# Scores of four pairs of heads in one burst of TensorE, and a new order of steps

## Chip, cores and metric

One core of one Trainium2 chip runs the whole program. The metric is the device time of one execution in microseconds (us).

## What is computed

Four layers in a row over x of shape (8, 1024, 256), fp32, each with a residual and a plain layer norm in front:

```python
x = x + attention_block(layernorm(x))   # 16 heads of 16, window of 128; inside: layer norm, qkv, attention, w_o, then an MLP with gelu
x = x + rwkv_ffn(layernorm(x))          # sigmoid(xr Wr) * (relu(xk Wk)^2 Wv)
x = x + mamba(layernorm(x))             # in_proj, causal conv of 4 taps, silu, selective scan over 16 states of 512 channels, gate, out_proj
x = x + top1_moe(layernorm(x))          # one of 8 experts for each of the 8 sequences, 256 -> 1024 -> 256
```

The change touches the sliding-window attention. With chunks of 128 rows, queries of a chunk see the keys of the chunk before and of their own:

```python
scores = jnp.einsum('bhcqd,bhckd->bhcqk', qc, kcat) * scale   # 128 x 256 for each head and chunk
scores = jnp.where(valid, scores, -inf)                       # band mask
attn = softmax(scores); out = einsum('bhcqk,bhckd->bhcqd', attn, vcat)
```

## The kernel before

The 8 sequences are cut in two groups of 512 tokens, so 16 groups `i` pass through the stages head, attention, mlp, rwkv, middle (what stands ahead of the scan), scan, back (out_proj and norm), route, fetch (weights of the expert from HBM) and expert. Groups overlap: while group i is in attention, i-1 is in mlp, rwkv and middle, i-2 in scan, i-3 in back and i-4 in expert.

Every engine has a generator for each stage, cut in steps by `yield`. `run` goes through one list, `order`, and lets each engine do its part of each step. So the order of work is the same on all five instruction queues, and only semaphores hold an engine back. The list comes from `schedule` (line 114): `COSTS` gives each step a length, `THREADS` places chains of stages in a time counted in slots (one group a slot), with `lag`, begin and end; all steps are sorted by that time. `SCAN_PERIOD` is the number of scan steps in a slot: the scan has `SCAN_STEPS` = 145 of them, one tile every two steps, so scans of neighbouring groups overlap a little.

`banks_of` (line 142) then goes through the order and gives each use of a PSUM bank (`uses_of`: name, first and last step) the bank that has been idle longest. There are 8 banks. PE waits for a bank with `free(use)`, readers wait with `full(use)`, and `gone(use)` says that it was read.

Attention has 72 beats from step `ATT0` = 14. A group has 4 chunks of 8 pairs of heads, 32 pairs n. Pair p of a chunk has its queries and keys in rows 32*(p%4) to 32*(p%4)+31 of `q_own` and `kT`, so a score matmul has 32 rows of contraction; `q_own` holds each pair twice, with the other head's rows zero (`par` 0 and 1). Before, `scores_of(v)` (line 487) makes pairs 2v and 2v+1 at beat 4v, in two banks: four matmuls, par 0 of both and then par 1 of both (line 499). On VectorE `masked(n)` (line 1065, the instruction stands at line 1074) adds the band, writes `prob` and the row's maximum and gives the bank back; at beats 4v+1 and 4v+2. ScalarE's `exponentials` (line 791) follow, then PE turns the probabilities (`turn`, line 511), ScalarE copies them (line 783), PE makes the values (line 527), and GpSimd's `divide` (line 1420). `prob` has a ring of 3 slots: `masked(n)` waits until `turn(n - 3)` is done.

The scan: SP loads a tile of u (line 1620, ring of 12 slots) and of delta (line 1607, ring of 5), each 256 KB, at step 2k + 10 + `LOAD_AT`; POOL multiplies by B (line 1499, `INPUT_AT`), ACT makes the decay in a bank (line 962, `DECAY_AT`), DVE scans (line 1287), POOL multiplies by C (line 1506, `OUT_AT`), and PE sums four tiles at once (line 670) at `SUM_AT`. `load_u(k)` waits until the sums of tile k - 12 are done, `load_delta(k)` until the decay of tile k - 5 is. u and delta come from the middle stage by way of DRAM: SP stores them (`store_delta`, lines 1577 and 1579) in middle's steps 22, 24, 26 and 28, in the same queue as the loads; each store waits for DVE's product (line 1255) and ACT's copy (line 937). At the start of mlp, PE transposes normed rows (`zb`, line 460), ACT copies them (`nb`, line 749) and PE makes the hidden rows (line 466).

## Time and profile before

| | |
|---|---|
| runs (us) | 3621.44, 3627.49, 10848.22; median 3627.49 |
| profiled execution (us) | 3620.18 |
| its span from first to last instruction (us) | 3618.1 |
| mean granted clock of TensorE | 0.910 of full speed |
| instructions | 58031 |
| DMA | 736.59 MB, mean 204 GB/s |

A row of a group of instructions names line, engine, operation, tiles written and read, shapes and count; then busy time in us (overlapping instructions counted once), mean length of one in ns, and the engine's idle time just before them with what ended most of it. PE is TensorE's matmul side, PEld its weight loads, DVE is VectorE, ACT ScalarE, POOL GpSimd, SP SyncE, which issues all DMAs of this kernel. An fp32 matmul stands in the trace as two MATMUL instructions. The chain of work that ended last is followed back from the last instruction, at each step to what released it.

### The profile page before, as it was taken

Reading aid. Unit: us, or ns where it says so; the run is one execution under the profiler, and the core shown is the slowest. Engines: PE = TensorE matmul, PEld = TensorE weight load, DVE = VectorE, ACT = ScalarE, POOL = GpSimd, SP = SyncE. Lnnn points to the kernel's source line nnn. Section 1 sums busy time; section 2 is a strip of 40 time slices with the busy share of each in tenths; the row PEclk is TensorE's granted clock in tenths of the full one; section 3 lists DMA queues with packets and bytes.
Section 4 is the critical chain, followed back from the end, with each engine's and each line's share of the span. In section 5 each row is a group of like instructions: output and inputs, shape, how many; then the busy total and the mean of one; then the engine's idle time right before and its main releaser. Section 6 shows DMA issues by size and latency. Waiting matters only on the chain.

```text
span 3618.1 us, 58031 instructions
## 1 busy us (share of the span) xinstructions
PE 3042.8 (84%) x17392; PEld 1885.8 (52%) x17392; DVE 2583.2 (71%) x5920; ACT 2415.5 (67%) x5331; POOL 2786.8 (77%) x2583
## 2 busy tenths in 40 slices
PE   5888888897988979899898989889898998987557
PEld 3555454464655646465464646556464654644236
DVE  3356878687787868778686876878687776878870
ACT  4577767676776857677685767768576776855431
POOL 1117989898887979888897988889798888977880
PEclk9998898899999989999898989989898998988678
DMA  2017877877777877877777887778878778789981
GB/s 73 7 42 192 214 208 193 225 215 238 207 204 222 217 229 216 241 209 204 223 218 228 220 237 210 207 222 226 230 215 234 210 204 231 213 248 256 284 235 37
DMA packets 423337, 736.59 MB, mean 204 GB/s; under 512 B 53427, under 2 KB 100147, under 8 KB 423027
## 3 DMA queue, kind: packets, MB, share of 16 engines
q1 hardware_dynamic: 423026, 732.89, 72.3%
q8 instruction: 142, 2.33, 0.3%
q14 instruction: 169, 1.38, 0.1%
HBM read 648.84 MB, written 83.89 MB: 203 GB/s over the span
## 4 chain that ended last, share of the span: by engine, by line
PE 60%; ACT 9%; POOL 9%; DVE 9%; issue 6%; DMA 5%; SPq 2%; ACTq 0%; DVEq 0%; POOLq 0%
PE bank L466 16%; PE bank L474 9%; PE bank L589 6%; PE bank L499 6%; PE bank L736 5%; PE bank L722 5%; PE bank L511 5%; POOL u_rows L1506 4%; PE bank L670 4%; DMA u_rows<-u_dram 3%; PE bank L527 3%; POOL u_rows L1499 3%; DVE u_rows L1287 3%; ACT prob L791 2%; DMA d_rows<-delta_dram 1%
## 5 line engine op out<-in xcount | busy, mean ns | idle before, releaser
L1506 POOL TENSOR_TENSOR u_rows<-u_rows,c_rows 128x512 f32<-128x512 f32 x1024 | 1304.8, 1277 | 169.3 <-DVE state L1292 116.4
L1499 POOL TENSOR_TENSOR u_rows<-u_rows,b_rows 128x512 f32<-128x512 f32 x960 | 1225.8, 1278 | 71.8 <-DMA u_rows<-u_dram 70.8
L962 ACT ACTIVATE bank<-d_rows,a_rep 128x512 f32<-128x512 f32 x1024 | 697.7, 688 | 296.5 <-DMA d_rows<-delta_dram 150.6
L1287 DVE TENSOR_TENSOR_SCAN u_rows<-bank,state,u_rows 128x512 f32<-128x512 f32 x512 | 644.0, 1271 | 83.3 <-ACT bank L962 78.9
L1287 DVE TENSOR_TENSOR_SCAN u_rows<-bank,u_rows 128x512 f32<-128x512 f32 x512 | 622.8, 1216 | 85.0 <-ACT bank L962 81.2
L791 ACT ACTIVATE prob<-prob,neg_max 128x256 f32<-128x256 f32 x1024 | 509.9, 505 | 42.9 <-DVE neg_max L1074 42.7
L670 PE MATMUL bank<-u_rows,sum_n 128*32 128x512 f32 x2048 | 309.1, 679 | 237.9 <-POOL u_rows L1506 235.0
L1074 DVE CUSTOM_DVE_ANT_0 prob<-bank,band 128x256 f32<-128x256 f32 x896 | 337.6, 416 | 178.0 <-PE bank L499 159.8
L511 PE MATMUL bank<-ident,prob 128*128 128x128 f32 x2048 | 330.3, 290 | 89.0 <-ACT prob L791 70.8
L511 PEld LDWEIGHTS bank<-ident,prob 128*128 128x128 f32 x2048 | 247.0, 148 | 230.8 <-issue 185.1
L499 PE MATMUL bank<-kT,q_own 32*128 32x256 f32 x2048 | 299.9, 412 | 47.4 <-DVE neg_max L1074 25.1
L466 PE MATMUL bank<-nb,w 128*128 128x512 f32 x512 | 271.1, 663 | 63.9 <-ACT nb L749 63.9
L499 PEld LDWEIGHTS bank<-kT,q_own 32*128 32x128 f32 x2048 | 181.9, 190 | 186.4 <-issue 135.7
L722 PE MATMUL bank<-y4T,w 128*128 128x256 f32 x1024 | 256.8, 398 | 10.7 <-DMA e_b<-in_b 9.6
L783 ACT ACTIVATE nT<-bank 128x512 f32<-128x512 f32 x256 | 151.2, 591 | 166.6 <-PE bank L527 128.3
L466 PE MATMUL bank<-nb,w_in 128*128 128x512 f32 x512 | 246.4, 609 | 15.0 <-DVE u_rows L1287 6.2
L736 PE MATMUL bank<-w,eT 128*128 128x256 f32 x1024 | 236.3, 384 | 6.3 <-ACT eT L1024 6.2
L722 PEld LDWEIGHTS bank<-y4T,w 128*128 128x128 f32 x1024 | 195.7, 200 | 67.1 <-issue 19.9
L589 PE MATMUL bank<-w,region_b 128*128 128x256 f32 x1024 | 230.4, 381 | 0.0
L670 PEld LDWEIGHTS bank<-u_rows,sum_n 128*32 128x32 f32 x2048 | 42.6, 113 | 352.8 <-POOL u_rows L1506 267.3
L736 PEld LDWEIGHTS bank<-w,eT 128*128 128x128 f32 x1024 | 191.3, 190 | 62.0 <-issue 33.7
L466 PEld LDWEIGHTS bank<-nb,w 128*128 128x128 f32 x512 | 103.3, 212 | 203.3 <-issue 134.6
(167 smaller groups left out, 5276.4 us busy)
## 6 DMA issues: line engine op xcount, KB each, us to landing
u_rows<-u_dram SPq DMA_DIRECT2D x1024, 256.0 KB, 5.4
d_rows<-delta_dram SPq DMA_DIRECT2D x1024, 256.0 KB, 5.1
w<-in_W SPq DMA_DIRECT2D x28, 1024.0 KB, 7.2
zs_dram<-region_b SPq DMA_DIRECT2D x64, 256.0 KB, 2.8
xc_dram<-region_b SPq DMA_DIRECT2D x64, 256.0 KB, 2.5
u_dram<-region_b SPq DMA_DIRECT2D x64, 256.0 KB, 3.4
delta_dram<-region_b SPq DMA_DIRECT2D x64, 256.0 KB, 3.1
yg<-xc_dram SPq DMA_DIRECT2D x64, 256.0 KB, 4.9
```

The lines of the kernel that those rows point to most:

```text
L466: ins = e.matmul(banks[use.bank][0:rows, :], lhsT(n), rhs(n), start=(n == 0), stop=(n == parts - 1))
L499: ins = e.matmul(banks[at.bank][:, 256 * par:256 * par + 256], q_own[rows, k, par, c * P:(c + 1) * P], kT[rows, k, c * P:(c + 2) * P], sta ...
L511: ins = e.transpose(banks[at.bank][:, (2 * par + half) * P:(2 * par + half + 1) * P], prob[:, n % PROBS, par, half * P:(half + 1) * P], id ...
L589: ins = e.matmul(banks[at.bank][:, 0:D], hT[:, k, t * P:(t + 1) * P], w_2[:, k, :], start=(k == 0), stop=(k == KF - 1))
L670: ins = e.matmul(banks[at.bank][32 * q:32 * q + 32, :], sum_n[:, r, :], rows_of(i, 4 * b + q), start=(r == 0), stop=(r == 3), skip_group_c ...
L722: ins = e.matmul(banks[at.bank][:, m % 2 * 256:m % 2 * 256 + 256], w_1[:, n, m * P:(m + 1) * P], y4T[:, n, t0:t0 + 256], start=(n == 0), s ...
L736: ins = e.matmul(out, eT[:, k, j * P:(j + 1) * P], w_2[:, k, :], start=(k == 0), stop=(k == KM - 1))
L791: ins = e.activation(tile, tile, ACT.Exp, scale=-1.0, bias=neg_max[:, c % 2, h:h + 1], accum_out=den[:, c % 2, h:h + 1])
L962: e.activation(banks[at.bank][:, :], delta_of(i, k), ACT.Exp, scale=a_rep[:, j:j + 1]).then_inc(filled[at.bank], 1)
L1287: e.tensor_tensor_scan(rows, banks[at.bank][:, :], rows, state[:, k:k + 1] if i % 2 else 0.0, ALU.mult, ALU.add).then_inc(drained[at.bank], 1)
L1499: e.tensor_tensor(rows, rows, b_rows[:, :], ALU.mult).then_inc(bx_ready.sem, 1)
L1506: e.tensor_tensor(rows, rows, c_rows[:, :], ALU.mult).then_inc(hc_ready.sem, 1)
```

## The change

`scores_of(u)` now makes four pairs 4u to 4u+3 at beat 8u, in four row groups and four banks: eight matmuls, par 0 of the four and then par 1. The masks of the four stand at beats 1, 2, 3 and 6 behind it (`MASK_AT`). `schedule` and `banks_of` become one function: at each turn it takes the earliest step whose banks are idle and whose chain's forerunners are through, so a step that needs more banks than are idle is put behind others. The costs of steps, the places of the chains and three numbers of the scan (`SCAN_PERIOD`, `LOAD_AT`, `SUM_AT`) are new. Instructions, sizes and buffers are otherwise the same.

```diff
--- before.py
+++ after.py
@@ -37,36 +37,37 @@
 
 
 ATT0, PROBS, TURNED, QUAD = 14, 3, 4, 4
+MASK_AT = (1, 2, 3, 6)
 AFTER = ATT0 + 72
 
 
 TILES = 64
-SCAN0, LOAD_AT, INPUT_AT, DECAY_AT, KEEP_AT, OUT_AT, SUM_AT, GATE_AT = 10, -9, -4, -2, 1, 3, 6, 8
+SCAN0, LOAD_AT, INPUT_AT, DECAY_AT, KEEP_AT, OUT_AT, SUM_AT, GATE_AT = 10, -10, -4, -2, 1, 3, 7, 8
 GATE_LOAD_AT = 14
 SCAN_STEPS = SCAN0 + 2 * (TILES - 1) + GATE_AT + 1
 
-SCAN_PERIOD = 133
+SCAN_PERIOD = 136
 COSTS = {
     "head": [2] * 6,
-    "attention": [1.5] * 2 + [0.8] * (ATT0 - 2) + [1] * (AFTER - ATT0) + [1.5] + [2] * 4,
-    "mlp": [1.5] * 2 + [1] * 16 + [4] + [1] * 8 + [2.5] * 3,
+    "attention": [1.5] * 2 + [0.8] * (ATT0 - 2) + [1] * (AFTER - ATT0) + [1.5] + [1.57] * 4,
+    "mlp": [1.5] * 2 + [1] * 8 + [1.31] * 8 + [4] + [0.92] * 8 + [1.75] * 3,
     "rwkv": [1.5] * 5 + [1] * 11 + [1.5] + [2.5] * 3,
     "middle": [1.5] * 2 + [1] * 27,
     "scan": [1] * SCAN_STEPS,
-    "back": [1.5, 1, 1, 1, 1, 1.5, 1.5, 1.5, 1, 1],
+    "back": [2.5] + [1] * 4 + [1.5] * 3 + [1] * 2,
     "route": [1] * 3,
     "fetch": [1],
-    "expert": [1] * 25,
+    "expert": [1] * 12 + [1.06] * 13,
 }
 
 
 THREADS = (
     (("head", "attention"), 0, 0.0, 1.0),
     (("mlp", "rwkv", "middle"), 1, 0.0, 1.0),
-    (("scan",), 2, 0.05, 0.05 + SCAN_STEPS / SCAN_PERIOD),
-    (("back",), 3, 0.16, 0.35),
-    (("route",), 3, 0.36, 0.39),
-    (("fetch",), 4, 0.39, 0.40),
+    (("scan",), 2, 0.034, 0.034 + SCAN_STEPS / SCAN_PERIOD),
+    (("back",), 3, 0.173, 0.368),
+    (("route",), 3, 0.378, 0.408),
+    (("fetch",), 4, 0.408, 0.418),
     (("expert",), 4, 0.44, 0.97),
 )
 
@@ -84,7 +85,7 @@
         for n in range(32):
             v, odd = divmod(n, 2)
             at = ATT0 + 4 * v
-            out += [(f"s{n}", at, at + 1 + odd), (f"p{n}", at + 5 + odd, at + 6 + 2 * odd)]
+            out += [(f"s{n}", ATT0 + 8 * (n // 4), ATT0 + 8 * (n // 4) + MASK_AT[n % 4]), (f"p{n}", at + 5 + odd, at + 6 + 2 * odd)]
             if n % 4 == 0:
                 out.append((f"a{n // 4}", ATT0 + 2 * n + 13, ATT0 + 2 * n + 14))
         return out + [("o0", AFTER, AFTER + 1), ("o1", AFTER, AFTER + 1)]
@@ -111,35 +112,32 @@
     return []
 
 
+class Use:
+
+
+
+    def __init__(self, bank, n, f):
+        self.bank, self.n, self.f = bank, n, f
+
+
 def schedule(batches):
 
-    at = []
+
+
+    chains = {}
     for thread, (stages, lag, begin, end) in enumerate(THREADS):
         total = sum(sum(COSTS[stage]) for stage in stages)
         for i in range(2 * batches):
-            spent = 0.0
+            chain, spent = [], 0.0
             for stage in stages:
-                if stage == "route":
-                    if i % 2 == 0:
-                        continue
-                    which = i // 2
-                else:
-                    which = i
+                if stage == "route" and i % 2 == 0:
+                    continue
+                which = i // 2 if stage == "route" else i
                 for step, cost in enumerate(COSTS[stage]):
-                    at.append((i + lag + begin + (end - begin) * spent / total, thread, stage, which, step))
+                    chain.append((i + lag + begin + (end - begin) * spent / total, thread, stage, which, step))
                     spent += cost
-    return [(stage, which, step) for _, _, stage, which, step in sorted(at, key=lambda s: s[:2])]
-
-
-class Use:
-
-
-
-    def __init__(self, bank, n, f):
-        self.bank, self.n, self.f = bank, n, f
-
-
-def banks_of(order, batches):
+            if chain:
+                chains[thread, i] = chain
 
     begins, ends = {}, {}
     for stage in COSTS:
@@ -147,17 +145,37 @@
             for name, first, last in uses_of(stage, shared):
                 begins.setdefault((stage, shared, first), []).append(name)
                 ends.setdefault((stage, shared, last), []).append(name)
-    idle, counted, signalled, uses = list(range(8)), [0] * 8, [0] * 8, {}
-    for stage, i, step in order:
-        shared = stage == "scan" and shared_inputs(i, batches)
-        for name in begins.get((stage, shared, step), ()):
+
+    def earlier(thread, i):
+
+        out = [] if THREADS[thread][0] == ("scan",) else [(thread, i - 1)]
+        if thread:
+            out.append((thread - 1, i | 1 if THREADS[thread][0] == ("fetch",) else i))
+        return out
+
+    order, uses = [], {}
+    idle, counted, signalled = list(range(8)), [0] * 8, [0] * 8
+    while chains:
+        for key, chain in sorted(chains.items(), key=lambda c: c[1][0][:2]):
+            _, _, stage, i, step = chain[0]
+            shared = stage == "scan" and shared_inputs(i, batches)
+            names = begins.get((stage, shared, step), ())
+            if len(names) <= len(idle) and not any(c in chains for c in earlier(*key)):
+                break
+        else:
+            raise AssertionError("no bank is idle")
+        order.append((stage, i, step))
+        for name in names:
             bank = idle.pop(0)
             uses[stage, i, name] = Use(bank, counted[bank], signalled[bank])
             counted[bank] += 1
             signalled[bank] += not (stage == "scan" and name[0] == "y")
         for name in ends.get((stage, shared, step), ()):
             idle.append(uses[stage, i, name].bank)
-    return uses
+        del chain[0]
+        if not chain:
+            del chains[key]
+    return order, uses
 
 
 def build_block_stack(nc, d):
@@ -184,8 +202,7 @@
     EL = P // NS
     assert WINDOW == P and SEQ % G == 0 and HD == 16 and GROUPS == 2 and ED // EL == TILES and KE * 16 == TILES
 
-    order = schedule(BATCH)
-    uses = banks_of(order, BATCH)
+    order, uses = schedule(BATCH)
 
     with ExitStack() as ctx:
         def sb(name, shape, dt=F32):
@@ -484,15 +501,15 @@
             def use(name):
                 return uses["attention", i, name]
 
-            def scores_of(v):
-
-                if v == 0:
+            def scores_of(u):
+
+                if u == 0:
                     for name in ("q0", "q1", "k0", "k1"):
                         e.wait_ge(*gone(use(name)))
-                for n in (2 * v, 2 * v + 1):
+                for n in range(4 * u, 4 * u + 4):
                     e.wait_ge(*free(use(f"s{n}")))
                 for par in range(2):
-                    for n in (2 * v, 2 * v + 1):
+                    for n in range(4 * u, 4 * u + 4):
                         c, p = divmod(n, PAIRS)
                         k, q = divmod(p, 4)
                         at, rows = use(f"s{n}"), slice(32 * q, 32 * q + 32)
@@ -548,8 +565,8 @@
                 yield
                 yield
             for beat in range(AFTER - ATT0):
-                if beat % 4 == 0 and beat < 64:
-                    scores_of(beat // 4)
+                if beat % 8 == 0 and beat < 64:
+                    scores_of(beat // 8)
                 v, at = divmod(beat - 5, 4)
                 if at < 2 and 0 <= v < 16:
                     turn(2 * v + at)
@@ -1105,9 +1122,9 @@
                 if n == 0:
                     yield
             for beat in range(AFTER - ATT0):
-                v, at = divmod(beat, 4)
-                if at in (1, 2) and v < 16:
-                    masked(2 * v + at - 1)
+                u, at = divmod(beat, 8)
+                if at in MASK_AT and u < 8:
+                    masked(4 * u + MASK_AT.index(at))
                 if beat % 8 == 2 and beat >= 10 and beat < 72:
                     reciprocals((beat - 10) // 8)
                 yield
```

## Rows read from the trace of the kernel before

**Rows 1.** The page: span, and busy time (share of it) and instructions of each engine

```profile
span 3618.1 us, 58031 instructions
...
PE 3042.8 (84%) x17392; PEld 1885.8 (52%) x17392; DVE 2583.2 (71%) x5920; ACT 2415.5 (67%) x5331; POOL 2786.8 (77%) x2583
```

**Rows 2.** Busy time by stretch (us), two whole periods

```profile
core 0: us, PE busy (x) PEld busy (x) DVE busy (x) ACT busy (x) POOL busy (x), PEclk, DMA share, GB/s
1773.00:1985.00 212.00, 186.74 (x1086) 116.61 (x1085) 159.11 (x339) 150.22 (x333) 178.94 (x167) 0.93 0.76 219
1985.00:2196.00 211.00, 188.02 (x1095) 117.04 (x1095) 158.11 (x391) 150.21 (x333) 178.32 (x163) 0.93 0.80 221
```

**Rows 3.** Busy time by stretch, one period: while scores are made, and the rest

```profile
1139.00:1253.00 114.00, 105.71 (x743) 73.17 (x744) 94.83 (x270) 86.22 (x228) 101.19 (x95) 0.96 0.81 217
1253.00:1351.00 98.00, 78.44 (x345) 42.29 (x345) 63.22 (x121) 63.86 (x106) 76.26 (x68) 0.90 0.73 221
```

**Rows 4.** Chain that ended last, by line: stretch 1139 to 1253, then the whole span

```profile
by line: PE bank L499 12.4%; PE bank L589 12.3%; PE bank L722 11.2%; PE bank L511 10.3%; PE bank L466 9.5%; PE bank L527 6.9%; PE bank L736 6.5%; PE bank L474 6.4%; PE bank L670 6.1%; issue 4.5%; ACT prob L791 2.3%; ACT region_b L879 2.0%; 
...
by line: PE bank L466 15.6%; PE bank L474 9.1%; issue 6.3%; PE bank L589 6.2%; PE bank L499 5.5%; PE bank L736 5.2%; PE bank L722 4.9%; PE bank L511 4.5%; POOL u_rows L1506 4.1%; PE bank L670 3.8%; DMA u_rows<-u_dram 3.3%; PE bank L527 3.3%
```

**Rows 5.** Timeline of PE (start us, us, what): one score step, whole and by starts

```profile
1194.14 1.13 PE L499 MATMUL bank<-kT,q_own 32*128 32x256 f32 x8
...
1194.46 0.38 PE L499 MATMUL bank<-kT,q_own 32*128 32x256 f32 x2
...
1194.68 0.38 PE L499 MATMUL bank<-kT,q_own 32*128 32x256 f32 x2
...
1194.89 0.38 PE L499 MATMUL bank<-kT,q_own 32*128 32x256 f32 x2
...
1195.20 0.33 PE L511 MATMUL bank<-ident,prob 128*128 128x128 f32 x1
```

**Rows 6.** Groups of instructions by form: score matmuls and masks

```profile
L499 PE MATMUL bank<-kT,q_own 32*128 32x256 f32 x2048 | 299.9, 412 | 47.4 <-DVE neg_max L1074 25.1 <-ACT z L800 11.2 <-DVE u_rows L1287 10.9
...
L1074 DVE CUSTOM_DVE_ANT_0 prob<-bank,band 128x256 f32<-128x256 f32 x896 | 337.6, 416 | 178.0 <-PE bank L499 159.8 <-PE bank L511 17.0 <-issue 0.3
```

**Rows 7.** Waits (engine line <- whom: us in total, times, longest us)

```profile
PE bank L670 <- POOL u_rows L1506: 235.0, 59, 9.2
...
DVE prob L1074 <- PE bank L499: 167.5, 99, 5.7
...
PE bank L466 <- ACT nb L749: 63.9, 16, 7.0
...
PE bank L499 <- DVE neg_max L1074: 25.1, 14, 1.9
```

**Rows 8.** Timeline where PE stops once a period; last row is the last period's

```profile
1300.90 1.94 PE L670 MATMUL bank<-u_rows,sum_n 128*32 128x512 f32 x8 [9.20 <-POOL u_rows L1506]
1302.77 1.68 PE L460 MATMUL bank<-ident,zb 128*128 128x128 f32 x8
1311.48 3.75 PE L466 MATMUL bank<-nb,w 128*128 128x512 f32 x4 [7.04 <-ACT nb L749]
...
1309.33 0.69 ACT L962 ACTIVATE bank<-d_rows,a_rep 128x512 f32<-128x512 f32 x1 [6.17 <-DMA d_rows<-delta_dram]
1309.96 1.43 ACT L749 ACTIVATE nb<-bank,vecs 128x512 f32<-128x512 f32 x2
...
3200.69 1.94 PE L670 MATMUL bank<-u_rows,sum_n 128*32 128x512 f32 x8 [9.00 <-POOL u_rows L1506]
```

**Rows 9.** Timeline of SP at that place: the last store and the loads behind

```profile
1303.14 0.46 SPq L1579 DMA_DIRECT2D delta_dram<-region_b  x1
1303.64 0.71 SPq L1620 DMA_DIRECT2D u_rows<-u_dram  x1
1304.39 0.64 SPq L1607 DMA_DIRECT2D d_rows<-delta_dram  x1
```

**Rows 10.** DMA issues: count, KB each, median us from issue to landing

```profile
w<-in_W SPq DMA_DIRECT2D x28, 1024.0 KB, 7.2
```

## The prediction

> **What bounds the kernel now.** I read the page first, then busy time by stretch over whole periods, then the chain of work that ended last inside one stretch, then the waits by line, and last the engines' order of work around the one place where all of them stop.
>
> The page shows no engine that is full: PE is busy 84% of 3618.1 us, POOL 77%, DVE 71%, ACT 67% [rows 1]. The kernel is a steady pipeline: from the fifth group on, one period (one group of 512 tokens enters, one leaves) lasts 211 to 212 us, and in it PE is busy 186.7 to 188.0 us and POOL 178.3 to 178.9 [rows 2]. So PE could give at most 9 us a period before POOL has as much to do as PE; both are 85 to 89% busy. In the stretch in which attention makes its scores (114 us of the period) PE is busy 105.7 us, 93%, and POOL 101.2, 89%; in the other 98 us PE is at 78.4 and POOL at 76.3 [rows 3]. The chain agrees: it runs through PE for most of the score stretch, and line 499, the score matmul, holds 12.4% of these 114 us; over the whole span it is 5.5% [rows 4]. That is where the change acts, and PE is what it acts on.
>
> **The score matmuls.** One step of two pairs now is four matmuls, eight instructions in the trace (each fp32 matmul has two). They start two by two, at 1194.14, 1194.46, 1194.68 and 1194.89, and the next line's work starts at 1195.20 [rows 5]. So two row groups already run side by side; the passes are 0.215 us apart, the first one takes 0.32 (its weights aren't there yet) and 0.31 passes between the last start and the next line. Sum 0.32 + 2 x 0.215 + 0.31 = 1.06 us a step, 16 steps in a group, 17.0 us. The change issues four pairs, one in each row group and each in a bank of its own, parity by parity: again four passes, now of four matmuls. If they run side by side as two do, a step still costs 1.06 us and there are 8, which takes 8.5 us from PE per group. Bounds: if four went no faster than two by two, a step would be 0.32 + 6 x 0.215 + 0.31 = 1.92 (eight passes have seven gaps, the first being 0.32) and the saving 17.0 - 15.4 = 1.6 us. I take the full overlap, since with two groups the two of a pass start together and the pass gets no longer for it than the gap of 0.215 us.
>
> The Trainium skill weighs against the full overlap: "TensorE: Matmul & The Clock Gate" (section Measured speedup vs the span model) has four row tiles at 3.07 times one, so a pass of four would last 1.3 times a pass of one. By an estimate from that figure two gaps of 0.28 and a last one of 0.37 make a step 1.25 us, the saving 7.0 us a group, and the forecast below 3537 instead of 3519. No trace here shows four row groups.
>
> Not all of the 8.5 us is on the path: of the 17.0 us of these steps the chain holds 12.4% of 114 = 14.1 us, 83%. So 8.5 x 0.83 = 7.1 us a group. The first two groups run while the pipeline fills and PE waits for others, so I count 14: -99 us. POOL goes with it: in a score stretch shortened from 114 to 107 us its 101.2 us would be 95%. I take a quarter of the gain back for that, +25; the bounds are nothing, and all of it.
>
> **The masks (DVE) and the banks.** The 32 masks of a group stay as they are (416 ns each half [rows 6]), at beats 1, 2, 3, 6 of 8 instead of 1, 2, 5, 6. Exponentials, turns and values don't move. DVE now waits 167.5 us for line 499 [rows 7], so it is ahead of PE and a burst finds it free. What grows is how long the banks are held: per eight beats 1+2+3+6 = 12 bank-beats where there were 2 x (1+2) = 6, so 0.75 bank more in the score stretch, and four have to be free at once. Worked out from the order of before, the number of idle banks when a score step comes is 3 in 30 cases of 160, 4 in 60, 5 or 6 in 70; two sufficed. Now four are needed, so a fifth of the steps must be put later by the new planner, and after most of them no bank is left: the next stage's matmul meets a bank that was drained just before. PE now waits 25.1 us in all for a mask before a score step [rows 7]. I take 1 us more a group, +14; the lower end is nothing (PE is the last to come), the upper one that all idle time before line 499, 47.4 us [rows 6], doubles, so about 50.
>
> **The scan moves.** SCAN_PERIOD 136 and begin 0.034 put the last tiles of a scan earlier against the stage that writes the next one's input. SP's queue is in order. Positions in slots from the tables: SP's stores of delta and u for blocks 1, 2, 3 stand at 0.948, 0.969, 0.990 in both; the loads of tiles 61, 62, 63 of the scan before stood at 0.975, 0.990, 1.005 and now at 0.931, 0.946, 0.960. So two or three loads that stood behind stores now stand ahead of them. What this costs now: the store at 1303.14 waited for ACT, the loads behind it go out at 1303.64 and 1304.39 [rows 9], the decay of that tile starts only at 1309.33 after 6.17 us of waiting, and the two copies queued behind it on ACT (line 749) hold PE for 7.04 us [rows 8]. It happens once a period, 63.9 us in 16 times [rows 7]; with the copies' own 1.43 us [rows 8] left over, 63.9 - 16 x 1.43 = 41 us can go: -41. The second stop of PE there, 9.20 us before the sums (line 670) [rows 8], 9.0 to 9.2 us in each of the 11 periods from 1080 on, of which the second and the last stand in [rows 8], I leave: the sums it lets through are followed at once by transposes (line 460, 1302.77), whose input comes at the end of a serial way from the output product through statistics and normed rows, and I see nothing that shortens that way. What is late next, once the copies are not, is that same way.
>
> SUM_AT 7 gives POOL one more step before PE sums (about 1.5 us). It takes away ring slack: a u slot is reloaded at step 2k-10, its sum stands at 2k-11, where it was 2k-9 after 2k-12. From sum to use of the row there are 7 steps instead of 8, 10.9 us against about 5 for a load (1304.39 to 1309.33 [rows 8, 9]): covered, cost 0; without that cover it would be a wait of POOL in every fourth tile. The fetch of expert weights stands 0.032 slot ahead of their use instead of 0.05: 6.8 us against 7.2 [rows 10] to land. SP runs about two steps ahead of its place, 3 us, which covers it; if not, up to 1 us in 15 groups. The retuned costs of the other stages move steps by 0.01 to 0.02 slot and remove no work: 0, with 20 us either way.
>
> **The sum.** Profiled execution 3620 (span 3618.1 and 2 us around it; the median of the runs is 7 us above it, so I read both as one). 3620 - 99 + 25 + 14 - 41 = 3519, say 3520 us, 3% less than the median of 3627.
>
> **Rivals.**
>
> A. The gain goes off the path: POOL is the next to be full. For it: POOL is 89% busy in the score stretch, and PE waits 235.0 us for it at line 670 [rows 3, 7]. Against: outside of that place the chain hardly touches it. If POOL takes three quarters of the 99 and the boundary stays, 3620 - 25 + 0 = 3595.
>
> B. Slower: bank shortage. Place: a matmul that needs the bank of a burst's last mask, which stands on DVE behind the burst's three others, 3 x 2 x 0.416 = 2.5 us [rows 6]. It decides once the mean new wait is over 7.1 / 8 = 0.9 us a score step; at 2.5 us, 8 steps and 14 groups, +280 against -99: 3800. For it: the fifth of the steps that lack a bank, and DVE 83% busy in that stretch. Against: 25.1 us now, and the planner puts steps later rather than let PE stand. The skill's "TensorEngine Tiling (Array Packing)" (PSUM Bottleneck) says that after a fourfold gain on TensorE evacuation may become the limit; by the rows DVE and ACT still have 17 and 24% of that stretch free (94.8 and 86.2 us busy of 114 [rows 3]).
>
> C. Four row groups don't run side by side. By the upper bound the saving is 1.6 us x 0.83 x 14 = 19: 3620 - 19 + 14 - 41 = 3574.
>
> D. The boundary goes too: both stops of PE (9.2 and 4.8 us) vanish and the saving on the scores is not given back: 3620 - 99 - 11 x 14 = 3367, with a part of it 3420.
>
> **How the numbers follow.** Forecast 0.50 (own range 3450 to 3570), A 0.20, B 0.10, C 0.08, D 0.12. The range that leaves out B and the far end of D is 3410 to 3625. A measurement tells about 2% from no change, so faster is below 3555: nearly all of D, 0.42 of the forecast's 0.50, a fifth of A, a fourth of C: 0.60. Slower (over 3700) is B, 0.09. The rest is 0.31.
>
> **What would show it.** Right: score steps as 16 instructions in 1.06 to 1.1 us with passes 0.215 us apart, busy time of line 499 near 150 us instead of 299.9 [rows 6], its share of the chain near 3%; periods of about 205 us; the wait of line 466 for line 749 at a third of 63.9 us, with the last loads of a scan ahead of the stores in SP's queue. Wrong: passes at 0.28 us or more (C); line 670 waiting longer than 235.0 us (A); PE waits on line 1074 of some 100 us (B); no 9 us stop before line 670 (D). The least sure step is how much of PE's saving the others let through.

## The result

The changed kernel takes 3596.6 us (median; 3593.0 to 3605.2) against 3627.5 of the kernel before, both on one chip: ratio 0.994, with a 95% interval of 0.991 to 0.997. That ratio is 21 us of 3620 (the medians differ by 31, the ratio is one of means) where the forecast took off 101 (3620 to 3519). The time lies inside the stated range (3410 to 3625) and outside the forecast's own one (3450 to 3570). One run of the kernel before, of 10848 us, stands in its median and not in the ratio. All ratios below are of this kind, each to the kernel before timed beside it; times are medians.

The page of the changed kernel, its span and its busy times:

```profile
span 3601.1 us, 58031 instructions
...
PE 2899.0 (81%) x17392; PEld 1794.3 (50%) x17392; DVE 2577.9 (72%) x5920; ACT 2432.3 (68%) x5331; POOL 2789.9 (77%) x2583
```

PE has 143.8 us less to do than in [rows 1], and the span is only 17.0 us shorter. So PE idles 127 us more. Busy time by stretch says that this happens in every period (columns as in [rows 2]; two whole periods, then one cut into the stretch of scores and the rest, as in [rows 3]):

```profile
1752.00:1963.00 211.00, 178.05 (x1087) 110.80 (x1086) 156.39 (x340) 151.75 (x334) 178.03 (x167) 0.94 0.78 220
1963.00:2175.00 212.00, 178.40 (x1093) 110.84 (x1091) 160.23 (x389) 151.94 (x335) 180.64 (x164) 0.94 0.80 219
...
1120.00:1237.00 117.00, 100.38 (x747) 69.27 (x747) 94.47 (x260) 84.90 (x219) 101.37 (x94) 0.94 0.80 214
1237.00:1332.00 95.00, 78.08 (x346) 41.64 (x346) 66.00 (x130) 67.01 (x116) 78.97 (x71) 0.93 0.77 227
```

PE's work in a period fell by 9 us, from 187 to 178, and the period stayed at 211 to 212 us. The score stretch got longer, 117 us for 114, though PE has 5 us less to do in it. All that the span gained, it gained while the pipeline fills: the score stretch shown begins at 1139 us before and at 1120 now, 19 us earlier, and at the end it is 17.

The score matmuls do what was forecast. Timeline of PE at one burst, whole and by starts:

```profile
1120.35 1.15 PE L516 MATMUL bank<-kT,q_own 32*128 32x256 f32 x16
...
1120.67 0.61 PE L516 MATMUL bank<-kT,q_own 32*128 32x256 f32 x8
...
1120.89 0.61 PE L516 MATMUL bank<-kT,q_own 32*128 32x256 f32 x8
...
1121.11 0.39 PE L516 MATMUL bank<-kT,q_own 32*128 32x256 f32 x4
1121.43 0.48 PE L491 MATMUL bank<-w_out,yg 128*128 128x256 f32 x1
```

The passes start at 1120.35, 1120.67, 1120.89 and 1121.11, and the next line at 1121.43: 1.08 us for sixteen instructions, where [rows 5] has 1.06 us for eight. By form, matmuls, masks and decays (as in [rows 6]):

```profile
L516 PE MATMUL bank<-kT,q_own 32*128 32x256 f32 x2048 | 152.9, 413 | 57.1 <-DVE u_rows L1304 45.0 <-ACT zb L909 9.3 <-ACT nb L764 2.1
...
L1091 DVE CUSTOM_DVE_ANT_0 prob<-bank,band 128x256 f32<-128x256 f32 x896 | 338.1, 416 | 214.2 <-PE bank L516 131.0 <-PE bank L528 82.2
...
L979 ACT ACTIVATE bank<-d_rows,a_rep 128x512 f32<-128x512 f32 x1024 | 702.5, 691 | 378.9 <-DMA d_rows<-delta_dram 183.7 <-DVE yg L1318 53.4 <-DVE u_rows L1304 49.4
```

Busy time of the score line is halved, 152.9 for 299.9 us. But PE now idles 45.0 us before it for line 1304, the scan on DVE. A score matmul reads nothing of the scan: what it waits for is a bank that a decay held. The decays on ACT wait for banks in the same way: idle time before them is 378.9 us (296.5 before), and 49.4 and 53.4 us of it are for lines 1304 and 1318, which read banks and never write a decay's input. The waits for the DMA are 183.7 us of it (150.6 before).

The largest part of PE's new idle time, 81 us, stands before the turns of the probabilities, line 511 before and 528 now:

```profile
L511 PE MATMUL bank<-ident,prob 128*128 128x128 f32 x2048 | 330.3, 290 | 89.0 <-ACT prob L791 70.8 <-ACT x L783 14.7 <-DVE u_rows L1287 2.7
...
L528 PE MATMUL bank<-ident,prob 128*128 128x128 f32 x2048 | 332.4, 289 | 170.4 <-ACT prob L808 85.4 <-DVE u_rows L1304 28.2 <-ACT eT L1041 14.8
```

PE is sooner done with the scores and then waits for the exponentials (line 808), whose steps did not move, and for banks. Waits by line (as in [rows 7]):

```profile
PE bank L477 <- ACT zb L773: 175.0, 17, 11.4
...
PE bank L687 <- POOL u_rows L1523: 89.7, 26, 10.5
DVE prob L1091 <- PE bank L528: 83.9, 84, 4.0
...
PE bank L483 <- ACT nb L766: 1.8, 2, 0.9
```

Line 687 is 670 of before and 477 is 460. Of the two stops once a period, that before the sums fell from 235.0 to 89.7 us and that for the copies of line 749 from 63.9 to 1.8. In their place stands a new one, 175.0 us (before 16.5), for the normed rows:

```profile
1292.47 1.97 PE L477 MATMUL bank<-ident,zb 128*128 128x128 f32 x8 [11.27 <-ACT zb L773]
```

The three together: 315 us before, 267 after.

### The profile page after: what moved, and what is told of

It is laid out like the page before. It is cut to its first block, busy times and chain, and to the rows that moved or that the text cites. A ratio compares the mean times of both kernels' runs of the same rounds, so it can differ in the third digit from the quotient of the medians.

```text
span 3601.1 us, 58031 instructions
## 1 busy us (share of the span) xinstructions
PE 2899.0 (81%) x17392; PEld 1794.3 (50%) x17392; DVE 2577.9 (72%) x5920; ACT 2432.3 (68%) x5331; POOL 2789.9 (77%) x2583
## 4 chain that ended last, share of the span: by engine, by line
PE 57%; DVE 14%; POOL 9%; ACT 9%; issue 8%; DMA 2%; SPq 1%; DVEq 0%; ACTq 0%; POOLq 0%
PE bank L483 16%; PE bank L491 9%; PE bank L739 5%; PE bank L687 5%; DVE u_rows L1304 5%; PE bank L606 5%; PE bank L753 4%; POOL u_rows L1523 4%; PE bank L528 4%; POOL u_rows L1516 3%; PE bank L516 3%; PE bank L544 2%; ACT prob L808 2%; PE bank L477 2%; DMA u_rows<-u_dram 2%
## 5 line engine op out<-in xcount | busy, mean ns | idle before, releaser
L979 ACT ACTIVATE bank<-d_rows,a_rep 128x512 f32<-128x512 f32 x1024 | 702.5, 691 | 378.9 <-DMA d_rows<-delta_dram 183.7
L1304 DVE TENSOR_TENSOR_SCAN u_rows<-bank,state,u_rows 128x512 f32<-128x512 f32 x512 | 643.9, 1271 | 83.9 <-ACT bank L979 83.3
L687 PE MATMUL bank<-u_rows,sum_n 128*32 128x512 f32 x2048 | 308.4, 678 | 91.4 <-POOL u_rows L1523 89.7
L483 PE MATMUL bank<-nb,w_in 128*128 128x512 f32 x512 | 260.5, 633 | 58.5 <-ACT nT L800 26.6
L753 PE MATMUL bank<-w,eT 128*128 128x256 f32 x1024 | 250.3, 402 | 6.0 <-ACT eT L1041 6.0
L483 PE MATMUL bank<-nb,w 128*128 128x512 f32 x512 | 245.5, 614 | 2.7 <-ACT nb L766 1.8
L753 PEld LDWEIGHTS bank<-w,eT 128*128 128x128 f32 x1024 | 205.3, 205 | 40.9 <-issue 12.0
L477 PE MATMUL bank<-ident,zb 128*128 128x128 f32 x384 | 74.0, 351 | 180.2 <-ACT zb L773 175.0
L606 PEld LDWEIGHTS bank<-w,region_b 128*128 128x128 f32 x1024 | 190.8, 191 | 41.3 <-issue 15.9
L1041 ACT ACTIVATE eT<-bank,e_b 128x256 f32<-128x256 f32 x256 | 107.3, 474 | 145.5 <-PE bank L739 145.5
L808 ACT ACTIVATION_READ_ACCUMULATOR prob<-prob,neg_max 128x1 f32 x1024 | 201.3, 197 | 0.0
L516 PE MATMUL bank<-kT,q_own 32*128 32x256 f32 x2048 | 152.9, 413 | 57.1 <-DVE u_rows L1304 45.0
```

What stands on the lines that cost most here:

```text
L483: ins = e.matmul(banks[use.bank][0:rows, :], lhsT(n), rhs(n), start=(n == 0), stop=(n == parts - 1))
L606: ins = e.matmul(banks[at.bank][:, 0:D], hT[:, k, t * P:(t + 1) * P], w_2[:, k, :], start=(k == 0), stop=(k == KF - 1))
L687: ins = e.matmul(banks[at.bank][32 * q:32 * q + 32, :], sum_n[:, r, :], rows_of(i, 4 * b + q), start=(r == 0), stop=(r == 3), skip_group_c ...
L753: ins = e.matmul(out, eT[:, k, j * P:(j + 1) * P], w_2[:, k, :], start=(k == 0), stop=(k == KM - 1))
L808: ins = e.activation(tile, tile, ACT.Exp, scale=-1.0, bias=neg_max[:, c % 2, h:h + 1], accum_out=den[:, c % 2, h:h + 1])
L979: e.activation(banks[at.bank][:, :], delta_of(i, k), ACT.Exp, scale=a_rep[:, j:j + 1]).then_inc(filled[at.bank], 1)
```

## The experiments

Each was timed in three rounds beside the kernel before, except e5 (one). The kernel before stands at 3613 to 3617 us in these, against 3627 above, so the ratios are what is compared.

**e1: order inside the burst.**

```diff
-                for par in range(2):
-                    for n in range(4 * u, 4 * u + 4):
+                for par, n in ((par, 4 * u + 2 * half + j) for half in range(2) for par in range(2) for j in range(2)):
```

> The changed kernel with one edit: the eight score matmuls of a burst run as two times four in two row groups, in the same place of the same order. PE has 8.5 us more to do in each group, the busy time of the score line goes from 152.9 back to about 300 us. Theory 1 (the path still runs through PE in the score stretch, the gain was lost elsewhere by the new places): the time rises by about 0.8 x 8.5 x 14 = 95 us, to 3690. Theory 2 (PE's score time is no longer on the path, DVE and ACT have taken its place): it rises by less than 30 us.

3601.5 us, ratio 0.996 (0.994 to 0.998), the same as the changed kernel. It doesn't test what it was made for: the row of the score line says that PE didn't get longer work.

```profile
L515 PE MATMUL bank<-kT,q_own 32*128 32x256 f32 x2048 | 156.5, 417 | 58.1 <-DVE u_rows L1303 45.9 <-ACT zb L908 9.3 <-ACT nb L763 2.0
```

156.5 us instead of the 300 expected: the matmuls of the second two row groups run beside those of the first two, even when all of the first two's are issued ahead of them. What a saving on PE is worth had to be asked in another way (e11, e12, e7 against e8).

**e2 and e3: the burst and the new times apart.** e2 is the changed kernel with the tables of before:

```diff
-SCAN0, LOAD_AT, INPUT_AT, DECAY_AT, KEEP_AT, OUT_AT, SUM_AT, GATE_AT = 10, -10, -4, -2, 1, 3, 7, 8
-SCAN_PERIOD = 136
+SCAN0, LOAD_AT, INPUT_AT, DECAY_AT, KEEP_AT, OUT_AT, SUM_AT, GATE_AT = 10, -9, -4, -2, 1, 3, 6, 8
+SCAN_PERIOD = 133
...
```

> The changed kernel (bursts of four, new masks' beats, new planner) with the costs, chain places, SCAN_PERIOD 133, LOAD_AT -9 and SUM_AT 6 of the kernel before. Theory 1 (the new places cost what the bursts gave): faster than the changed kernel, 3520 to 3560, with the two stops of PE (9 and 5 us) once a period back. Theory 2 (bursts of four lack banks in any order): slower than the changed kernel, 3640 or more. If the new places are worth what the bursts are, it stands at 3600 to 3630.

e3 is the changed kernel with the steps and masks of before:

```diff
-            out += [(f"s{n}", ATT0 + 8 * (n // 4), ATT0 + 8 * (n // 4) + MASK_AT[n % 4]), ...
+            out += [(f"s{n}", at, at + 1 + odd), ...
-                if beat % 8 == 0 and beat < 64:
-                    scores_of(beat // 8)
+                if beat % 4 == 0 and beat < 64:
+                    scores_of(beat // 4)
...
```

> The changed kernel's costs, places, scan numbers and planner, with the score steps and masks of before (two pairs each four beats). Score line busy 300 us. Theory 1 (the new places cost time by themselves): slower than before, 3650 to 3700. Theory 2 (the places are neutral or better, the burst is what costs): about 3600 or less, below the kernel before. The L670 stop of 9 us should be gone in either.

e2 takes 3685.2 us, ratio 1.019 (1.015 to 1.022); e3 takes 3527.7, ratio 0.976 (0.974 to 0.978). The burst, with all that goes with it, costs some 70 us with either tables (e2 against before 68, the changed kernel against e3 69), and the tables give some 90 with either steps. The change is the sum of a loss and a gain, and e3, without the burst that the change is named for, beats both kernels. The new planner has no part in it: with the numbers and steps of before it gives the list of steps and the banks of before, step by step. The stops once a period are not what the burst costs: e3 has them as the changed kernel has (192.1 us for the normed rows, 87.1 before the sums).

Part of what the tables give may come by TensorE's clock, which the prediction did not look at. Busy time and granted clock around the two stops of the kernel before (columns as in [rows 2]):

```profile
1290.00:1300.00 10.00, 1.70 (x10) 0.29 (x2) 9.86 (x23) 5.38 (x10) 9.63 (x10) 0.69 0.78 243
1300.00:1310.00 10.00, 3.55 (x16) 1.65 (x16) 7.28 (x20) 3.83 (x9) 4.67 (x5) 0.67 1.07 360
1310.00:1320.00 10.00, 8.52 (x18) 3.10 (x18) 6.71 (x16) 7.09 (x13) 9.75 (x10) 0.62 0.97 319
1320.00:1330.00 10.00, 9.84 (x38) 4.16 (x34) 4.05 (x6) 6.70 (x12) 9.92 (x11) 1.00 0.48 136
```

PE stands for 9.20 and then 7.04 us, and the granted clock is 0.62 in the stretch behind it, between the two levels of 1.2 and 2.4 GHz. Four matmuls of line 466 at 1311.48 take 3.75 us there [rows 8]; four of the same line take 1.88 at 1325.66, at a clock of 1.00. The two groups that run behind the stops, in the kernel before and in e3:

```profile
L466 PE MATMUL bank<-nb,w 128*128 128x512 f32 x512 | 271.1, 663 | 63.9 <-ACT nb L749 63.9
L659 PE MATMUL bank<-dbc,pick_b 96*128 96x512 f32 x64 | 44.9, 791 | 1.0 <-DVE u_rows L1287 0.9
...
L483 PE MATMUL bank<-nb,w 128*128 128x512 f32 x512 | 245.5, 615 | 4.1 <-ACT nb L766 2.1 <-issue 0.9 <-DVE u_rows L1304 0.8
L676 PE MATMUL bank<-dbc,pick_b 96*128 96x512 f32 x64 | 36.1, 647 | 0.0
```

With the same instructions PE is busy 2988.6 us in e3 and 3042.8 before, 54 us less, at a mean granted clock of 0.926 for 0.910. These two groups are 34 of the 54, and 18 more are the products with `w_x`, which run elsewhere in the period (602 ns for 756). PE's idle time fell by 40 us besides. How much of the 54 reaches the time isn't separated by any run.

**e5: is POOL the next limit?**

```diff
-                e.tensor_tensor(rows, rows, b_rows[:, :], ALU.mult).then_inc(bx_ready.sem, 1)
+                e.tensor_tensor(rows[:, 0:G // 2], rows[:, 0:G // 2], b_rows[:, 0:G // 2], ALU.mult).then_inc(bx_ready.sem, 1)
```

(and the same for the product by C)

> The changed kernel with both products of the scan on POOL (by B and by C) made on the first 256 of 512 columns only; the rest of the columns is left out, so part of the computation is missing. POOL loses some 35 to 40 percent of its work, about 65 us a period. If POOL (178 to 181 us busy of 212) sets the period, the time falls by more than 300 us. If the period is set by handovers between PE, DVE and ACT, it falls by less than 100 us.

3548.7 us, ratio 0.982 (0.978 to 0.985):

```profile
PE 2870.6 (81%) x17392; PEld 1771.5 (50%) x17392; DVE 2542.7 (72%) x5920; ACT 2430.7 (69%) x5331; POOL 1730.7 (49%) x2583
```

1059 us of POOL's work are gone, 38% of it, and the time falls by 1.3% against the changed kernel (0.982 / 0.994), some 45 us. POOL's length isn't what holds the period. Rival A falls, though its number, 3595, is the one that was measured: that is luck. Its sign, a longer wait than 235.0 us before the sums, did not show (89.7).

**e11 and e12: what PE's score time is worth.** Half of the score columns left out, in the kernel before and in e3:

```diff
-                        ins = e.matmul(banks[at.bank][:, 256 * par:256 * par + 256],
-                                       q_own[rows, k, par, c * P:(c + 1) * P], kT[rows, k, c * P:(c + 2) * P],
+                        ins = e.matmul(banks[at.bank][:, 256 * par:256 * par + 128],
+                                       q_own[rows, k, par, c * P:(c + 1) * P], kT[rows, k, c * P:(c + 1) * P],
```

> The kernel before; each score matmul makes the first 128 of its 256 columns only (the other half of the scores is left out), so PE has 16 x 4 x 0.107 = 6.9 us less to do in each group and nothing else changes: same list of steps, same banks. It measures what PE's score time is worth by itself. If the chain's share (12.4 percent of the score stretch) is what a saving returns, 0.83 x 6.9 x 14 = 80 us come back, 3535. If handovers in the fixed order set the period, less than 30 us.

> The same cut (half of the score columns left out, 6.9 us less on PE in each group) in kernel e3 (new times, pair steps, 3528 us). If PE's time is on the path there, 3450 to 3470; if it is not, as e1 said for the changed kernel, 3500 to 3528.

e11 takes 3599.8 us against 3615.7, ratio 0.995 (0.993 to 0.997); e12 takes 3505.4, ratio 0.968 (0.965 to 0.971) against 0.976 of e3. The row of e11:

```profile
L499 PE MATMUL bank<-kT,q_own 32*128 32x128 f32 x2048 | 190.6, 306 | 55.8 <-DVE neg_max L1074 24.6 <-DVE u_rows L1287 20.8 <-ACT z L800 10.4
```

PE lost 109 us of score time and the kernel 16 to 18: a sixth. In e3 it is 22 to 29 us, a fifth to a quarter. The chain had line 499 for 83% of its length in the score stretch. Busy times and the chain by engine, the kernel before and then e11:

```profile
PE 3042.8 (84%) x17392; PEld 1885.8 (52%) x17392; DVE 2583.2 (71%) x5920; ACT 2415.5 (67%) x5331; POOL 2786.8 (77%) x2583
PE 60%; ACT 9%; POOL 9%; DVE 9%; issue 6%; DMA 5%; SPq 2%; ACTq 0%; DVEq 0%; POOLq 0%
...
PE 2971.7 (83%) x17392; PEld 1865.7 (52%) x17392; DVE 2592.1 (72%) x5920; ACT 2414.2 (67%) x5331; POOL 2783.6 (78%) x2583
PE 51%; ACT 14%; DVE 13%; issue 8%; POOL 8%; DMA 5%; SPq 2%; DVEq 0%; ACTq 0%; POOLq 0%
```

Two things happened to the 109 us. First, PE as a whole is busy only 71 us less: the granted clock is 0.892 to 0.902 in all ten runs of e11 and 0.908 to 0.914 in those of the kernel before beside them, and the matmuls that were not touched got longer (the turns of line 511 from 290 to 297 ns, the expert's from 384 to 395). In e12 it is the same, 75 us for 112, at 0.913 for 0.926. Second, of the 71 us a quarter came back: the chain left PE for ACT and DVE.

**e7, e8, e13: banks.** e7 puts the third mask back; e8 is e3 with only the banks taken as for a burst:

```diff
-MASK_AT = (1, 2, 3, 6)
+MASK_AT = (1, 2, 5, 6)
```

> The changed kernel with the third mask of each burst back at beat 5 (masks at 1, 2, 5, 6 of 8, as before the change). The third bank is held 5 beats instead of 3, and the third mask follows three beats behind the turn of probabilities that it waits for instead of one. Theory B (banks: a bank is taken again too soon after it was given free) expects it to be slower than the changed kernel, by 10 to 40 us. Theory M (DVE stands at the early third mask, 83.9 us of waits for line 528 against 21.9 in the kernel with pair steps) expects it faster, by 40 to 70 us.

```diff
-            out += [(f"s{n}", at, at + 1 + odd), ...
+            out += [(f"s{n}", ATT0 + 8 * (n // 4), at + 1 + odd), ...
```

> The kernel e3 (new times, two pairs each four beats, 3528 us), in which the banks of four pairs are taken together at beat 8u, although the second two pairs are computed only at beat 8u + 4, where they were. Masks at 1, 2, 5, 6. The list of steps and the banks are those of e7; only the place of the second half of the score matmuls differs. Theory B: it loses what the burst loses, 3590 to 3630, with ACT's waits for banks at the decays up from some 70 us to 200. Theory M, or a theory that the burst itself disturbs PE: it stays within 20 us of 3528.

e7: 3607.2 us, ratio 0.997 (0.996 to 0.999). e8: 3625.7, ratio 1.002 (1.001 to 1.004), 2.6% above e3, 95 us. The matmuls, their places and the masks of e8 are those of e3; only the hold of banks is longer. Idle time before ACT's decays, e3 and then e8:

```profile
L979 ACT ACTIVATE bank<-d_rows,a_rep 128x512 f32<-128x512 f32 x1024 | 700.6, 690 | 261.6 <-DMA d_rows<-delta_dram 182.8 <-DVE region_b L1237 21.9 <-DVE x L1211 17.2
```

```profile
L979 ACT ACTIVATE bank<-d_rows,a_rep 128x512 f32<-128x512 f32 x1024 | 702.9, 692 | 372.7 <-DMA d_rows<-delta_dram 179.7 <-DVE u_rows L1304 46.5 <-DVE yg L1318 43.7
```

The wait for the DMA is the same; the 111 us more are for lines that give banks back. e7 has e8's list of steps and banks, with the matmuls in bursts: it is 0.5% faster, 18 us. That is what the burst's 153 us of score time are worth where banks are scarce; PE as a whole is busy 127 us less (2897.4 for 3024.2, at a granted clock of 0.914 for 0.922) and idles 58 us longer before the turns. The early third mask, which gives its bank back two beats sooner, is worth 0.3% (the changed kernel against e7), with intervals that overlap: it isn't told from nothing. It does show that the longer waits of DVE at this mask (83.9 us for line 528 above, 18.4 before and 59.1 in e7) aren't what the burst costs.

Holding banks does two things: the planner puts some steps later, and a bank is taken sooner after it was given back. Worked out from the lists, only 14 of 5736 steps of e8 go more than one place later, 14 of the 128 bursts' steps and by two places at most, and 24 steps of the expert stage go six places earlier. The second is large: in the steady part of e3 a decay takes a bank within three steps of its release in 11% of the cases and an attention use in 15%, in e8 in 25% and 37%. e13 makes the second alone:

```diff
-            bank = idle.pop(0)
+            bank = idle.pop(min(1, len(idle) - 1))
```

> Kernel e3 with the same list of steps and the same bank demand, but of the idle banks the second longest idle is taken, so that in effect seven banks circulate. A bank is then taken within three steps of its release in 27 percent of the scan's cases and 35 percent of attention's (e3: 11 and 15; e8, with banks held for bursts: 25 and 37). If the burst loses by waits for banks just released, this loses as much as e8: 3600 to 3630. If e8 lost by steps that the planner put later, this stays at 3528 to 3550.

3585.2 us, ratio 0.991 (0.988 to 0.993): 1.5% of e8's 2.6% with a list of steps identical to e3's. Its reuse within three steps is about as frequent as e8's (27% and 35%), so early reuse makes more than half of the loss. What makes up the rest (the moved steps, or which banks are met early) wasn't separated. Idle time before the decays is 376.6 us here and 372.7 in e8, with 40 us between the two kernels: it shows that banks are met early there, but it doesn't measure the loss.

**c4 and d2: the reverse.** The same edit on the changed kernel and on e3:

```diff
-SCAN0, LOAD_AT, INPUT_AT, DECAY_AT, KEEP_AT, OUT_AT, SUM_AT, GATE_AT = 10, -10, -4, -2, 1, 3, 7, 8
+SCAN0, LOAD_AT, INPUT_AT, DECAY_AT, KEEP_AT, OUT_AT, SUM_AT, GATE_AT = 10, -10, -4, -1, 1, 3, 7, 8
```

> The changed kernel with DECAY_AT -1 instead of -2: each of the scan's decays holds its bank one step instead of two, so the mean number of idle banks rises from 3.43 to 3.86, that of pair steps (3.81). The price is that ACT makes a decay only one step ahead of DVE's scan. If the burst's loss is bank shortage and the lead costs nothing, it comes back to 3530 to 3560; if the lead is worth as much as the bank, it stays at 3590 or is slower.

> e3 (pair steps, new times, 3528 us) with DECAY_AT -1, the control of c4, which gained 60 us on the changed kernel by the same edit. If the edit relieves only the burst, this stays at 3528 or is slower by up to 30 us, and the burst's loss is bank shortage. If it gains as much as c4 did, to 3470, the decay's place was bad for all and says nothing on the burst.

c4: 3534.1 us, ratio 0.978 (0.976 to 0.979), 1.7% or 60 us faster than the changed kernel. d2: 3538.0, ratio 0.980 (0.977 to 0.982), 0.4% slower than e3. So a shorter hold of the decays' banks pays with the burst and doesn't with pair steps: relief gives back about what shortage took. With relief, burst and pair steps are level (0.978 and 0.980).

**e9, e10, c1, c2, c3: what the tables gave.** Each adds a part of the new tables to the kernel before. e9 the scan's numbers, e10 all costs and the other places:

```diff
-SCAN0, LOAD_AT, INPUT_AT, DECAY_AT, KEEP_AT, OUT_AT, SUM_AT, GATE_AT = 10, -9, -4, -2, 1, 3, 6, 8
-SCAN_PERIOD = 133
-    (("scan",), 2, 0.05, 0.05 + SCAN_STEPS / SCAN_PERIOD),
+SCAN0, LOAD_AT, INPUT_AT, DECAY_AT, KEEP_AT, OUT_AT, SUM_AT, GATE_AT = 10, -10, -4, -2, 1, 3, 7, 8
+SCAN_PERIOD = 136
+    (("scan",), 2, 0.034, 0.034 + SCAN_STEPS / SCAN_PERIOD),
```

> The kernel before with the new planner and only the scan's numbers of the change: SCAN_PERIOD 136, begin 0.034, LOAD_AT -10, SUM_AT 7. Pair steps, masks, costs and other chains as before. If the 9 and 5 us stops of PE once a period were due to the scan's place against the stores (my step), it shows most of the 89 us that e3 gains on the kernel before: 3530 to 3560. If the retuned costs carry the gain, it stays near 3610.

> The kernel before with the new planner and only the new costs and the places of back, route and fetch; scan's numbers, pair steps and masks as before. My step said that these costs move nothing that counts: within 20 us of the kernel before. If they carry the gain of e3, it is at 3530 to 3560.

e9: 3651.9 us, ratio 1.010 (1.006 to 1.014), slower. e10: 3551.6, ratio 0.982 (0.979 to 0.986). In e9 the two stops go, as my step had it, and return as one for the normed rows, with more waits in the score stretch:

```profile
PE bank L477 <- ACT zb L773: 151.4, 27, 9.8
PE bank L687 <- POOL u_rows L1523: 96.1, 41, 9.5
PE bank L528 <- ACT prob L808: 81.9, 78, 2.6
...
PE bank L516 <- DVE u_rows L1304: 40.7, 15, 6.0
```

The costs, one part each:

```diff
-    "attention": [1.5] * 2 + [0.8] * (ATT0 - 2) + [1] * (AFTER - ATT0) + [1.5] + [2] * 4,
+    "attention": [1.5] * 2 + [0.8] * (ATT0 - 2) + [1] * (AFTER - ATT0) + [1.5] + [1.57] * 4,
```

> The kernel before (new planner, which gives the same list and banks with the old numbers) with one edit: attention's last four steps cost 1.57 each instead of 2. The output product moves from 0.910 to 0.913 of the slot and every beat gets 1.6 percent longer. If the gain of e10 (65 us) lies in the stretch of time given to the score beats, about 3570; else within 15 us of the kernel before.

> The kernel before with one edit: the costs of mlp (second half of the hidden rows 1.31, output products 0.92, last three steps 1.75). The hidden rows are each 1.9 us of PE between steps of others, so a longer cost there lets scan and attention steps come between. If this carries the gain of e10, 3550 to 3570; else within 15 us of the kernel before.

> The kernel before with one edit: the places of back, route and fetch and the costs inside back and expert. The out product of the scan moves from 0.184 to 0.211 of the slot, out of the dense start of attention. If this carries the gain of e10, 3550 to 3570; else within 15 us of the kernel before, or slower by a few us because the fetch stands 3.7 us nearer to the experts.

c1: 3523.7 us, ratio 0.975 (0.973 to 0.977). c2: 3583.9, 0.992 (0.990 to 0.995). c3: 3676.0, 1.017 (1.014 to 1.020). One number of one table is worth 92 us, as much as the whole set; the parts don't add up (c1, c2 and c3, which hold all of e10's numbers, would be 0.984 together and e10 is 0.982, but e9's numbers add 1.0% to before and take 0.6% off e10, which gives e3). Waits of c1:

```profile
PE bank L687 <- POOL u_rows L1523: 224.1, 55, 9.3
...
PE bank L483 <- ACT nb L766: 42.2, 16, 4.0
POOL x L1457 <- PE bank L544: 41.4, 14, 3.6
```

The stop before the sums is still there (224.1 for 235.0 us), so the gain isn't at that place. POOL's wait for the last values (line 1440 of before) fell to 41.4 from 122.1 us. Why 1.6% more of the slot for the beats does all this is not shown by any run. All three expectations missed: c1 gained twice what was named, c2 half of it, and c3 lost 60 us where a few were allowed for.

**e14 and d1: two attempts at more.** e14 begins the chain of mlp 0.03 slot later in e3; d1 puts DECAY_AT -1 into c1.

```diff
-    (("mlp", "rwkv", "middle"), 1, 0.0, 1.0),
+    (("mlp", "rwkv", "middle"), 1, 0.03, 1.0),
```

> Kernel e3 with the chain of mlp, rwkv and middle begun 0.03 slot (6 us) later and ending where it did. It puts other steps between the output product and the next transposes, where PE stands 11.1 us a period for the normed rows in e3. If that stop is a loss of its own, it falls to 5 to 7 us and the time by 40 to 70 us, to some 3470. If the same serial way only shows up elsewhere, the time stays within 15 us of 3528, or rises since the chain is pressed together.

```diff
-SCAN0, LOAD_AT, INPUT_AT, DECAY_AT, KEEP_AT, OUT_AT, SUM_AT, GATE_AT = 10, -9, -4, -2, 1, 3, 6, 8
+SCAN0, LOAD_AT, INPUT_AT, DECAY_AT, KEEP_AT, OUT_AT, SUM_AT, GATE_AT = 10, -9, -4, -1, 1, 3, 6, 8
```

> c1 (the kernel before with the last four costs of attention at 1.57, 3524 us) with DECAY_AT -1. If banks are scarce in pair steps too, it gains again and is the fastest kernel here, 3470 to 3500. If they are not, the shorter lead of ACT on DVE costs it something: 3520 to 3560.

e14: 3736.4 us, ratio 1.033 (1.028 to 1.037). The stop for the normed rows went from 192.1 us in e3 to 29.2, and that before the sums came up from 87.1 to 264.9. d1: 3569.4, ratio 0.989 (0.985 to 0.992), 1.4% slower than c1 and outside of both expected ranges: here the shorter hold doesn't pay at all. That it is ACT's shorter lead that costs is a reading; no run separates it.

## Why the prediction was wrong, step by step

The direction was right and the size off by a factor of five (101 us forecast, 21 measured), and that the small remainder has the right sign is the balance of two large terms, so in part luck. As a ledger in ratios, from neighbouring kernels that differ in one part of the change each:

| part | from | measured | forecast (us) |
|---|---|---|---|
| new tables | e3 against before | -2.4%, -87 us | -41 |
| banks held for four pairs | e8 against e3 | +2.6%, +95 us | +14 |
| matmuls in bursts | e7 against e8 | -0.5%, -18 us | -99 and +25 |
| third mask two beats sooner | changed kernel against e7 | -0.3%, -11 us (within the noise) | 0 |
| sum | | -0.6%, -21 us | -101 |

**The cost of a step: right.** Four row groups run beside each other at no cost to the pass, 1.08 us for 1.06, and the score line's busy time is 152.9 us where near 150 was forecast. The figure of the Trainium skill that I weighed ("TensorE: Matmul & The Clock Gate", Measured speedup vs the span model; 3.07 times for four row tiles, at 512 columns) isn't borne out for 256 columns in fp32: the pass spacing is 0.22 us with four as with two, where 0.28 was the estimate. Rival C falls.

**"8.5 x 0.83 = 7.1 us a group": the step that failed first.** I took the share of the chain as what a saving returns. e11 measured it on the very kernel that the chain was read from: 109 us taken from these matmuls returned 16 to 18, a sixth for 83%. Two causes show in its trace. The term had nothing for the granted clock, and 38 of the 109 us went back into the other matmuls at 0.897 for 0.910. And a chain names what ended last once: with the scores shorter, it runs through ACT and DVE for 27% of the span where it had 18. My reading, which no run tests by itself, is that where PE, DVE, ACT and POOL hand work on every few microseconds in one fixed list, another chain lies close beside the first. The rows had a sign: of the 25 us of a period in which PE waits, only 16 are the two stops, and some 8 are small pieces in the score stretch itself.

**The quarter given back to POOL: the wrong guard.** POOL at 95% looked like the next limit; e5 shows that 38% of its work can go for 1.3%.

**"I take 1 us more a group, +14": the bank term mis-sized by seven.** The mechanism stood in the text (0.75 bank more, 3 idle banks in a fifth of the cases) and I priced it by PE's waits at line 499 alone. Its price is 95 us (e8), and the waits came elsewhere: 111 us more idle time at ACT's decays, which take a bank each two steps, and 45 us more at PE's turns. Rival B had the cause and the wrong place: not behind the burst's own masks (DVE waits for PE there, PE waits 0.7 us for line 1091), but at every stage that takes a bank just given back. The Trainium skill says it in "TensorEngine Tiling (Array Packing)", Gotcha 1: row tiling increases PSUM pressure. The runs agree and give it a price here, 2.6%. Of the two things that I named, steps put later and a bank drained just before, e13 shows the second by itself to cost 1.5%, and the first is small. The fifth was misread besides: bursts stand at every second of the 160 steps counted, and of these 80 only 10 find 3 banks idle, an eighth.

**The scan's stops: mechanism right, value wrong.** The loads moved ahead of the stores (in the changed kernel the last load of the scan goes out at 1287.38, the last stores at 1293.08 and 1293.71), the wait for line 749 went from 63.9 to 1.8 us, and I had named what would be late next, the way to the normed rows. I should have taken nothing for it: in e9 the waits for the normed rows rise to 151.4 us and the scan's numbers alone lose 1.0%.

**"Remove no work: 0, with 20 us either way": wrong.** The costs and places by themselves gave 1.8% (e10), one of them 2.5% (c1), another part took 1.7% (c3). What no sum of waits would have had is the clock: in e3 the matmuls behind the stops are 34 us shorter, and all of PE's work 54. In a kernel whose list of steps is fixed, a number that removes no work can be worth more than the work that the change removes.

**Two sums.** Rival D's two stops are 9.2 and 4.8 us, 14.0 a period, and stand in its sum as 11 without the 41: it should read 3325 and not 3367. And the 3537 for slower passes leaves the 25 us for POOL as they are; a quarter of the smaller gain would be 20, and the time 3532. Neither moves the forecast.

## What to carry to other kernels

In a hand-made order shared by all engines, price a saving by taking the work out on the chip, not by its share of the chain, and read the engine's whole busy time and the granted clock beside it: here a third of what was taken from the scores came back in other matmuls. Count a bank by how long it is held and how soon it is taken again; the waits here rose most in a stage that has nothing to do with the scores. And time the parts of a change apart: here the part it is named for lost 2% and a cost of 1.57 instead of 2 (c1, 3524 us) or the tables with the old steps (e3, 3528 us) beats the kernel before by 2.5 or 2.4% and the changed one by 1.9 or 1.8%.

## What the hardware showed that I had not expected

Four row groups with 32 rows and 256 columns in fp32 cost what two cost, 1.08 against 1.06 us a step. And the order of issue inside a burst doesn't matter: in e1 both parities of two row groups come ahead of the other two groups, and the busy time of the line is 156.5 us against 152.9.
